# One queue of expert tiles for elements 0 to 5, results stored by indirect writes and fetched back at the end

## What is computed

```
x = x + rwkv(layernorm(x))     # time mixing (a scan over tokens), channel mixing
x = x + ffn(layernorm(x))      # attention of 16 heads, then a mixture of experts

# the second half of ffn, for the 512 tokens of an element:
m     = layernorm(x)
probs = softmax(m @ Wg)                        # 8 experts
wts, idx = top_k(probs, 2)                     # each token goes to two experts
wts = wts / sum(wts)
h1 = gelu(m @ W1[e] + b1[e]);  ye = h1 @ W2[e] + b2[e]
out = x + sum over the two chosen experts of wts * ye
```

## Time and profile before

| what | value |
|---|---|
| median of three runs | 981.35 us (979.06 to 991.71) |
| span of the profiled execution, which stands for its own time | 987.7 us |
| PE, DVE, ACT, POOL busy | 83%, 67%, 61%, 43% |
| last exponentials (end of element 7's scores) | 870.41 + 1.02 us |
| from there to the end of the span | 116.3 us |
| mean TensorE clock granted | 0.905 of 2.4 GHz |

### The profile page before, as it was taken

How to read it: one execution, slowest core, us unless ns; L and a number is a source line. 1 busy time by engine, 2 the same in 40 slices (tenths; PEclk the granted TensorE clock), 3 DMA queues, 4 the chain that set the end, 5 groups by cost and what they waited for, 6 DMA issues and landing times. The chain is left out here.

```text
span 987.7 us, 15981 instructions
## 1 busy us (share of the span) xinstructions
PE 820.5 (83%) x5416; PEld 516.9 (52%) x5416; DVE 665.6 (67%) x1341; ACT 600.2 (61%) x1016; POOL 424.9 (43%) x543
## 2 busy tenths in 40 slices
PE   3558898878898999788989998988898888898772
PEld 1444445434555654345556555654565555478771
DVE  4538858886879688868886878687867576223112
ACT  2123446644787687447876887677768876556341
POOL 5544333534553455464534553454556013115263
PEclk9675798888899999898999999998999998699797
DMA  6500321991522300015233321053223320558793
GB/s 196 169 12 9 122 98 49 292 347 45 179 90 89 101 21 9 12 33 180 89 100 103 108 86 57 30 183 97 89 80 123 119 80 27 181 188 298 236 309 95
DMA packets 106286, 116.77 MB, mean 118 GB/s; under 512 B 7983, under 2 KB 89310, under 8 KB 106206
## 3 DMA queue, kind: packets, MB, share of 16 engines
q1 hardware_dynamic: 102110, 107.36, 34.3%
q0 software_dynamic: 4096, 8.40, 2.6%
HBM read 77.24 MB, written 38.49 MB: 117 GB/s over the span
## 5 line engine op out<-in xcount | busy, mean ns | idle before, releaser
L1456 DVE TENSOR_REDUCE QA<-psB 128x2 f32<-128x1024 f32 x256 | 311.9, 1219 | 124.0 <-PE psB L1143 121.7
L943 ACT ACTIVATE PT<-psB 128x1024 f32<-128x1024 f32 x256 | 261.9, 1023 | 134.3 <-PE psB L1159 130.4
L1159 PE MATMUL psB<-Q,KT 32*128 32x512 f32 x512 | 134.4, 521 | 34.0 <-ACT PT L943 20.6
L1143 PE MATMUL psB<-KT,Q 24*128 24x512 f32 x512 | 136.9, 530 | 22.6 <-DVE QA L1456 21.7
L1171 PE MATMUL psV<-PT,VA 128*32 128x512 f32 x1024 | 148.5, 654 | 0.6
L1236 PE MATMUL psA<-MX,WB 128*128 128x128 f32 x792 | 109.4, 290 | 31.2 <-ACT H L971 19.7
L971 ACT ACTIVATE H<-psA,WB 128x128 f32<-128x128 f32 x396 | 109.8, 376 | 33.3 <-PE psA L1236 31.3
L1236 PEld LDWEIGHTS psA<-MX,WB 128*128 128x128 f32 x792 | 100.0, 202 | 39.4 <-issue 28.3
L1246 PEld LDWEIGHTS psY<-WB,H 128*128 128x128 f32 x792 | 96.8, 194 | 27.8 <-ACT H L971 16.8
L1159 PEld LDWEIGHTS psB<-Q,KT 32*128 32x128 f32 x512 | 49.7, 191 | 117.1 <-ACT PT L943 75.3
L1246 PE MATMUL psY<-WB,H 128*128 128x128 f32 x792 | 107.6, 282 | 0.0
(11 more groups left out here) (198 smaller groups left out, 1360.0 us busy)
## 6 DMA issues: line engine op xcount, KB each, us to landing
WB<-w_rows SPq DMA_DIRECT2D x99, 578.0 KB, 5.7
pairs<-XT SPq DMA_DIRECT2D x2, 5120.0 KB, 18.5
outs<-XT SPq DMA_DIRECT2D x2, 5120.0 KB, 33.5
XT<-pairs SPq DMA_DIRECT2D x99, 64.0 KB
outs<-YT SPq DMA_DIRECT2D x99, 64.0 KB
w_rows<-WB SPq DMA_DIRECT2D x8, 578.0 KB, 3.3
X<-in_L_attn_x_dram SPq DMA_DIRECT2D x8, 256.0 KB, 3.0
H<-in_L_ffn_W_dram SPq DMA_DIRECT2D x8, 256.0 KB, 3.9
```

The lines of the kernel that those rows point to most:

```text
L943: act.activation(PT[:, (c % 2) * G + j:(c % 2) * G + j + 2, :], psT, ACT.Exp, scale=SCALE).then_inc(t_taken.sem, 1)
L1143: pe.matmul(dst[:, h, :], chunk(Q1[r, g, :], c), KT[r, g, :], start=True, stop=True).then_inc(s_full.sem, 1)
L1159: pe.matmul(psT[:, h, :], chunk(KT[r, g, :], c), Q2[r, g % 2, :], start=True, stop=True).then_inc(t_full.sem, 1)
L1456: dve.tensor_reduce(QA[:, c, g * G + j:g * G + j + 2, RM], plain(b, i), AX_X, ALU.max).then_inc(s_taken.sem, 1)
```

## The change

Elements 0 to 5 form one group, [0..5], [6], [7]. A group's tiles are worked off in stages: after each member from the second on, the tiles that are surely full by then (8 for each member, less 7) are worked off, and all that is left after the last member. That makes 9 + 8 + 8 + 8 + 22 tiles for elements 0 to 5 and 15 each for elements 6 and 7, 85 tiles in 30 windows. A row in `pairs` now carries its own token number in front of it and behind it (130 values for 128), and the area is one of 257 blocks, cleared in eight pieces of 4 DMAs. Windows begin at slots given by hand: three a turn up to slot 216, seven in the turn of element 7's scores (slots 224 to 252), then element 6's five 4 apart from 256 and element 7's five from 280.

The output rows of a tile are scattered by token number, one indirect DMA of 128 rows a tile on GpSimd (L820's place is taken by L830 of the new kernel), into an area `results` in token order; VectorE makes the row numbers (`tile_places`, two small instructions a window). Each element is then fetched by two plain DMAs of 256 KB (SyncE, L599, into one buffer YG for each choice) and combined, elements 0 to 5 at slots 271 to 292, element 6 at 294, element 7 at 312.

```diff
-    MEMBERS = [[0]] + [[b, b + 1] for b in range(1, B - 1, 2)] + [[B - 1]]
+    MEMBERS = [list(range(B - 2)), [B - 2], [B - 1]]
+    for group, m in enumerate(MEMBERS):
+        given = 0
+        for i, b in enumerate(m):
+            known = 2 * T // TW * (i + 1) + (E - 1 if b == m[-1] else 1 - E)
+            if i or b == m[-1]:
+                STAGE[b] = len(TILES)
+                TILES.append(known - given)
...
-        YG = sb("YG", [P, 2, NT, 2, C])
+        YG = sb("YG", [P, 2, NT, C])
...
-    STRIDE = [8, 8, 8, 5, 8]
+        START = [SLOTS * (b + 1) + PER * AHEAD + PER * i for b in range(1, B - 3) for i in range(WIN)]
+        START += [216] + [224, 232, 236, 240, 244, 248, 252] + [256, 260, 264, 268, 272] + [280, 284, 288, 292, 296]
+        FETCH_AT = [267, 280, 282, 284, 286, 288, 290, 308]
+        COMBINE_AT = [271, 284, 286, 288, 290, 292, 294, 312]
+        STORE_AT = [282, 286, 288, 290, 292, 294, 297, 313]
...
+            def fetch_rows(b):
+                if b == MEMBERS[GROUP_OF[b]][0]:
+                    for w in range(LAST_WINDOW[GROUP_OF[b]] - 1, LAST_WINDOW[GROUP_OF[b]] + 1):
+                        sp.wait_ge(y_out[w % 2], moved(w))
+                for k in range(2):
+                    if b > 0:
+                        sp.wait_ge(*((combined.sem, combined.at(b - 1, 1)) if k else (dve_y, b)))
+                    first = (k * B + b) * T
+                    sp.dma_start(YG[:, k, :, :], TK[first:first + T, :].rearrange("(c p) n -> p c n", p=P)).then_inc(fetched[k], 16)
...
-            TILE = {3: (tile_step(0, next_rows),), 7: (tile_step(0, next_weights),), 9: (tile_step(0, rows_out),)}
+            TILE = {3: (tile_step(0, next_rows),), 7: (tile_step(0, next_weights),)}
...
+            def chunks_now(b, first):
+                if b < B - 1:
+                    return range(first, first + NT // 2)
+                return range(0 if first else NT)
...
+            def tile_out(first):
+                w = window(first)
+                pool.wait_ge(places.sem, places.at(w, 1))
+                pool.wait_ge(y_taken.sem, y_taken.at(w, 1))
+                for i in range(len(members(w))):
+                    pool.indirect_dma_start(TK, bass.IndirectOffsetOnAxis(IDT[:, w % 4, i:i + 1], 0),
+                                            YT[:, w % 2, i, :], None).then_inc(y_out[w % 2], 16)
+
+            OUT_AT = {24: 12, 0: 10, 8: 16}
+            TILE_OUT = [start + (OUT_AT[start % SLOTS] if w < WINDOW_0[STAGES - 3] else 11) for w, start in enumerate(START)]
...
-            END = {4: (gather(0, 0),), 8: (gather(0, 1), gather(0, 2),), 16: (gather(0, 3),), 17: (gather(1, 0),),
-                   31: (gather(1, 1),), 32: (gather(1, 2), gather(1, 3),)}
...
-            TILE = {10: (tile_step(0, tile_out),)}
+            TILE = {4: (tile_step(0, tile_places),), 10: (tile_step(0, tile_out),)}
-            POST = {7: (c_ctx,), 13.5: (c_norm,), 16: (c_gate,), 17: (c_top,), 18.5: (c_rank,), 22: (tile_map,)}
-            END = {30: (combine(0),), 46: (combine(1),)}
+            POST = {7: (c_ctx,), 13.5: (c_norm,), 16: (c_gate,), 17: (c_top,), 18.5: (c_rank,), 20.5: (tile_map,)}
...
+                    for b in range(B):
+                        if SLOTS * n + s == COMBINE_AT[b]:
+                            combine_rows(b)
```

More of the change, by code:

```diff
@@ L421, in build @@
         scattered = [[sem(f"scattered_{k}_{c}") for c in range(NT)] for k in range(2)]
-        gathered = [[sem(f"gathered_{k}_{c}") for c in range(NT)] for k in range(2)]
+        ids_ready = sig("ids_ready")
+        places = sig("places")
+        fetched = sem("fetched_0"), sem("fetched_1")
         combined = sig("combined")
@@ L465, in __call__, with tiles @@
                 self.step(n, *self.parts)
-        def tiles(n, at, table):
+        def tiles(n, at, table, end_table=None):
             for w, start in enumerate(START):
-                for step in table.get(SLOTS * n + at - start, ()):
+                now = end_table if end_table and window_stage(w) >= STAGES - 2 else table
+                for step in now.get(SLOTS * n + at - start, ()):
                     if step.which < len(members(w)):
@@ L834, in turn @@
                     for at in (s, s + 0.5):
+                        for w in range(len(START)):
+                            if SLOTS * n + at == TILE_OUT[w]:
+                                tile_out(members(w)[0])
                         extras(at, (role["post"], POST), (role["core"], CORE), (role["tail"], TAIL), (role["head"], HEAD))
-                    grouped(n, s, END, END_OF)
             over(turn)
@@ L1022, in keep_clock @@
                 for _ in range(WARM.get((name, b), 0)):
-                    pe.matmul(psT[:, 0, 0:P], ident[:, :], ones[:, :], start=True, stop=True)
+                    pe.matmul(psT[:, 0, 0:P], ident[:, :], ones[:, 0:P], start=True, stop=True)
             def head_rows(b):
@@ L1193, in c_norm @@
                 pe.wait_ge(zm_ready.sem, zm_ready.at(b, 1))
-                transposes(use(b, "rows").bank, ZM[:, b % 2, :, :]).then_inc(use(b, "rows").full, 1)
+                transposes(use(b, "rows").bank, ZM[:, b % 2, :, 1:C + 1]).then_inc(use(b, "rows").full, 1)
             def c_logits(b):
@@ L1207, in rank @@
                 for back in range(NT + 1):
-                    last = pe.matmul(dst[:, 0:(NT + 1) * E], ones[:, :] if back else lower[:, :],
+                    last = pe.matmul(dst[:, 0:(NT + 1) * E], ones[:, 0:P] if back else lower[:, :],
                                      SEL[:, NT - back:2 * NT + 1 - back, :].rearrange("p c e -> p (c e)"),
@@ L1536, in c_rank @@
             def c_rank(b):
-                i = MEMBERS[GROUP_OF[b]].index(b)
-                if i:
+                group = GROUP_OF[b]
+                first = b == MEMBERS[group][0]
+                if not first:
                     dve.wait_ge(use(b - 1, "rank").taken, use(b - 1, "rank").after)
@@ new lines, in tile_map @@
+                starts = TH[:, :].rearrange("p (e j) -> p e j", j=NB)[:, :, BLOCK_0[group]:BLOCK_0[group] + blocks]
+                own_t.begin(stage)
+                dve.wait_ge(use(b, "rank").taken, use(b, "rank").after)
+                count = POS[:, b % 2, NT, :].unsqueeze(2).to_broadcast([P, E, blocks])
+                own_t.link(dve.scalar_tensor_tensor(out=by_block(new), in0=count, scalar=0.0 if last else 1.0 - TW, in1=starts,
+                                                    op0=ALU.add, op1=ALU.is_gt))
@@ new lines, in tile_map @@
+                own_t.link(dve.scalar_tensor_tensor(out=by_block(place_of), in0=by_block(place_of), scalar=TQ[:, 0:1] if not first else 0.0,
+                                                    in1=by_block(added), op0=ALU.add, op1=ALU.mult))
+                dve.tensor_reduce(TQ[:, :], by_block(new), mybir.AxisListType.XY, ALU.add).then_inc(dve_q, 1)
+                own_t.link(dve.scalar_tensor_tensor(out=by_block(place_of), in0=by_block(place_of), scalar=TI[:, 0:1], in1=starts,
+                                                    op0=ALU.is_equal, op1=ALU.mult))
@@ new lines, in tile_map, with tile_places @@
+                own_t.end()
+            def tile_places(first):
+                w, size = window(first), len(members(window(first)))
+                dve.wait_ge(xt_in[w % 2], moved(w))
+                if w >= 4:
+                    dve.wait_ge(y_out[w % 2], moved(w - 4))
+                if w > 0:
+                    dve.wait_ge(places.sem, places.at(w - 1, 1))
+                own_p.begin(w)
+                own_p.link(dve.tensor_tensor(IDF[:, 0:size], XT[:, w % 2, 0:size, 0], XT[:, w % 2, 0:size, C + 1], ALU.min))
+                own_p.end()
+                dve.tensor_tensor(IDT[:, w % 4, 0:size], IDF[:, 0:size], AWAY[:, w % 2, 0:size], ALU.min).then_inc(places.sem, 1)
```

280 lines of the change are left out of this document (132 added, 148 removed).

## The result

The changed kernel takes 1024.2 us (median of 4 runs, 1021.6 to 1028.8) against 981.5 us beside it: a ratio of 1.042 (95% interval 1.038 to 1.046). The forecast was 1006 us with 1020 as the upper end, so the direction was right and the size was not: 43 us were lost where 24 had been counted. The profiled execution has a span of 1027.1 us against 987.7, 39.4 us more.

A forecast was written before the change was run, and what follows sets the result against it. It took the tail steps' chain through in-order queues to bound most turns, then waits for element 7's rows, weights and YT. Terms summed to +24.2 us, 1011.9 us by span; the median, 6.4 us lower, gave 1006 us, range 983 to 1020.

The forecast's parts named there:

- turns 0 to 6: Turns before element 7's scores: fewer windows and gathers against a longer start list, -2.7 us, bounds -8 and +10.
- element 7's scores: Turn of element 7's scores: more windows between exponentials cost 17.2 us, clock gives back 5; +12 us, bounds +5 and +18.
- last exponential to the rows' request: Element 7's way to its tiles: more PE tiles and a late gate, +7.5 us, bounds +1 and +10.
- rows' request to last YT: Element 7's windows: fetches and combinations delay the YTs, 58 us instead of 48.9, +9 us, bounds -8 and +16.
- the end: After the last YT: indirect stores, two fetches, combination and store, 16 us instead of 17.6; -1.6 us, bounds -3 and +1.
- the prediction's own sign: Sign that the forecast is wrong: turns 2 to 5 shorter than 96 us or longer than 101.
- the rival of the windows: Turns 2 to 6: expert windows set their length, five fewer at 6.1 us each give 30 us; chance 0.06.
- that of GpSimd's stores: Rival: stores and scatters in GpSimd's queue delay the norms 3 us in each of seven turns, +21 us; chance 0.08.
- The combination ahead of the gate: Element 7's way to its tiles: VectorE waits for element 0's fetch and combination, making the gate 6.3 us late.
- up to its gate PE does 9 tiles, where it did 8.6: +1 us: After the last exponentials, before element 7's gate: PE's extra tile work costs +1 us.
- nothing waits, five windows at PE's own pace, -8: Lower bound for element 7's windows: no waits, 7.0 us a window at PE's pace, -8 us.
- The third rival: Whole kernel: GpSimd's queued stores and scatters hold up the turns, +21 us, 1027 us; chance 0.08.

The follow-up runs named there:

- e11: Kernel before, with the third tile's output of group [5, 6] moved behind two of the next window's hidden rows: 990.0 us, ratio 1.008.
- e6: Changed kernel without fetching or combining elements 0 to 6, and with the third output ahead of the next window's hidden rows: 985.9 us, ratio 1.002.
- e8: Changed kernel with an exponential in place of the experts' gelu, removing the table loads between them: 1017.0 us, ratio 1.033 to the kernel before.
- e2: Changed kernel with element 0's fetch and combination moved behind element 7's gate, rank and tile map: 1015.2 us, ratio 1.031 to the kernel before.
- e1: Changed kernel with elements 0 to 6 neither fetched nor combined, only element 7: 1005.5 us, ratio 1.022 to the kernel before.
- e3: Changed kernel with a second buffer pair for the fetches, all slots unchanged: 1020.1 us, ratio 1.035 to the kernel before.
- e5: Changed kernel with the third output ahead of the next window's hidden rows in elements 6 and 7's windows: 1015.5 us, ratio 1.031.
- e4: Changed kernel with GpSimd's stores of the window at slot 264 moved ahead of element 7's scatter: 1028.5 us, ratio 1.045 to the kernel before.
- e10: Changed kernel with third output earlier, fetches 0 to 2 ahead, three buffer pairs, four of element 6's windows behind element 7's rank: 990.6 us, ratio 1.007.

## Why the prediction was wrong in size

By its own steps, changed kernel against the kernel before in the profiled executions:

| step | forecast | profiled | what the runs show |
|---|---|---|---|
| turns 0 to 6 | -2.7 | +3.5 | between -2 and +3, see below |
| element 7's scores | +12 | +8.4 | 3 more windows |
| last exponential to the rows' request | +7.5 | +11.0 | gate stall and order; the rank alone +15.7 |
| rows' request to last YT | +9 | +20.5 | loop and order |
| the end | -1.6 | -4.0 | |
| sum | +24.2 | +39.4 | |

**Turns 0 to 6.** Element 7's scores began at 785.7 us against 782.2. But the eleven other versions of the changed kernel, which are nearly the same up to there, began them between 774.9 and 783.3, the twelve together at a median of 780.1. Against 782.2 that is -2.1, near the forecast; but 782.2 is the draw of one execution too, and e11, which is the kernel before up to there, began them at 776.9, against which it is +3.2. So the sign of the term is open. What varies most is the first three turns: turn 2 took 97.8 to 103.6 us, and in the 103.6 us one the clock was 0.84.

By the prediction's own sign (turns 2 to 5 longer than 101 us) something was missed here: nine of the twelve have a turn 2 or 3 of 101.3 us or more. The two together took 199.1 to 203.7 us, median 200.8, where the kernel before and e11 had 197.0. No run shows why. Turns 4 to 6 took 294.0 to 297.2 us against 299.0 and 297.1. So the rival of the windows, 30 us less in turns 2 to 6, is not seen, and neither is that of GpSimd's stores, 3 us more in each turn; in e6 all the stores and scatters are there and nothing is lost.

**Element 7's scores.** Right in kind: the clock came back to 1.00 and three windows cost 8.4 us net, for a forecast of 12. PE was busy 84 us there, not 92. How the two parts share it can be read from e11, where the same scores with the windows of the kernel before took 83.0 us at a clock of 0.98: against that the three windows cost 14.6 us (4.9 us each, where 6.1 had been priced), and the clock gave back 6.3 us, for 5 assumed (one trace each). The table loads are on the path in part: e8 gave back 6.4 us for 14 of them. The drain that the Trainium skill gives ("ScalarE: Activation LUTs", "What ACT_TABLE_LOAD costs"), and by which the sum would have been 8 us higher, is not borne out by e8 either: the loads cost less than their own 1.28 us, not more.

**The way to the tiles.** The combination ahead of the gate was right in place and near in price: e2 gave back 9 us for a foretold 6.3; among the reasons is that fetch 0 was issued 6.7 us after YT and not 4.3. **What failed is the term beside it, "up to its gate PE does 9 tiles, where it did 8.6: +1 us".** e1, with no combination, still has the rank 9 us later than the kernel before. With the order put right (e6) it is 3.3 us later. In all the rank was 15.7 us late; the rows' request was so by 11.0 only, because it now follows the last scatter by 3.3 us, where it took 8.0 before. The prediction had nothing for that.

**Element 7's windows.** The same step failed again: the lower bound "nothing waits, five windows at PE's own pace, -8" was taken for what is left without fetches. From the last scatter to the last YT e1 has 22.3 + 38.8 us left, 5 us more than the 56.3 of the kernel before. With the order put right (e6) it is 48.5 us, 8 less. But 5 of these 8 are the earlier request: in the prediction's own count, from the rows' request to the end of the last YT, it is 45.8 us against 48.9, so that even then 3 us come back and not 8; in e1 it is 58.3. The loop of fetches itself is real, first YT 29.6 us after the rows' request for a forecast of 28.5; its cause is the place behind 3.5 MB of weights more than the one buffer (e3). What the forecast lacked is what follows: 39.8 us from there to the end of the last YT, where it had 29.5.

**The end.** 13.6 us from the end of the last YT, against 16 foretold and 17.6 before: two plain fetches in the place of eight gathers.

**The sum.** Of the 42.7 us between the medians the combinations account for 18.7 (e1) and the order for 19.6 more (e1 to e6); what is left is not to be told from the kernel before, the scores' 8.4 us being paid for by element 7's earlier request, shorter windows and end. The split hangs on what is taken out first: the order first gives 8.7 us (e5) and the combinations then 29.6 (e5 to e6), since the two cover each other. The forecast had the first at 16.5 us (7.5 + 9) and the second not at all, since PE's order in the last windows was not looked at: the prediction compared ScalarE's lists and took PE's for unchanged. The third rival came nearest to the measured time (1027 us for 1024.2), by another mechanism, which e6 excludes: GpSimd's stores are all in it. That it came near the number is chance.

## What to carry to other kernels

A ring of two windows prefetches only as long as nothing of window w stands behind an instruction of window w+1 that needs w+1's own load: read the order of the engine that consumes the weights, at the new spacing, before pricing a window at the engine's pace. When work is moved into an in-order queue ahead of a chain that sets the end, price the wait of its transfer, not its instructions; here 2.3 us of adding held the gate for 9. A long idle time in the waits view is a cost only if something later moves when it goes (e4).

## What the runs showed of the hardware that was not expected

- A fetch of 2 x 256 KB behind one window's weights and rows was used 4.2 us after its issue (914.54 to 918.79), behind two windows' 7.5 us (954.65 to 962.14): at equal size, what stood ahead on the queue made the difference.
- After a PE pause of 2.4 us in the changed kernel 16 matmuls took 3.53 us instead of 1.95 (granted clock 0.50 from 904 to 906). In e11, after a pause of 2.1 us, 8 matmuls still took 1.13 us and the next 8 took 2.05 (0.50 from 880 to 882). Both waits for weights were paid a second time in clock.
- With 1.7 MB of weights requested for a window, the hidden rows of its first tile started 4.4 to 4.6 us after issue. With the DMA engines busy throughout, e10 moved 329 GB/s over 40 us; for 2 us at a time the changed kernel moved 385 (904 to 906).
- The first three turns differ by 3.5 to 6 us each between the profiled executions of the twelve versions (turn 2: 97.8 to 103.6 us), the later ones by 1 to 2 us.
